# Pooling over rows: add two accumulators on the Vector engine first, then one set of matmuls in place of two

## What is computed

```python
def _forward(x, Wr, br, w1, b1, w2, b2, Wp1, bp1, Wp2, bp2):
    ...
    for e in range(E):                       # 12 experts, top 3 for each token
        ...
        out = out + mask[..., None].astype(x.dtype) * (w_e * h)
    pooled = out.mean(axis=1)                # mean over the 512 tokens of each batch
    phi = jax.nn.sigmoid(jax.nn.relu(pooled @ Wp1 + bp1) @ Wp2 + bp2)
    phi_mask = (phi > 0.7).astype(out.dtype)[:, :, None]
    return out * (1.0 - phi_mask * 0.8)
...
x = x + 0.5 * _L0_ffn_ref(_layernorm(x, axis=-1), ...)
x = x + _L0_attn_ref(_layernorm(x, axis=-1), ...)
x = x + 0.5 * _L0_ffn_ref(_layernorm(x, axis=-1), ...)
```

## Time and profile before

| | us |
|---|---|
| median of 3 runs | 842.14 |
| lowest and highest run | 838.91 to 844.8 |
| the profiled execution | 843.17 |
| its span, first to last instruction | 841.3 |
| PE busy | 695.0 (83% of the span) |
| DVE busy | 532.5 (63%) |

### The profile page before, as it was taken

The page is one execution under the profiler, slowest core; times in us unless marked ns, Lnnn a source line. Parts: engine busy times, 40 slices in busy tenths (PEclk is TensorE's granted clock), DMA queues, the critical chain, the costliest instruction groups (busy, mean ns, idle before and its releaser), DMA issues.

```text
span 841.3 us, 20947 instructions
## 1 busy us (share of the span) xinstructions
PE 695.0 (83%) x6530; PEld 589.0 (70%) x6531; DVE 532.5 (63%) x1085; ACT 313.9 (37%) x704; POOL 422.6 (50%) x302
## 2 busy tenths in 40 slices
PE   1416799999999998659999974179999999999964
PEld 1315687789889997238888863159999999989822
DVE  6895899745555555169899889835555555555505
ACT  3886677433333332022232221243333333333300
POOL 0003488888888885111100100137888888888520
PEclk9757999999999999769999995579999999999977
DMA  9987543656555654710000003043444444444473
GB/s 304 376 312 235 153 70 63 145 99 112 94 112 94 113 94 63 219 50 2 1 0 0 2 1 101 6 133 57 75 75 75 75 75 75 75 75 75 56 211 114
DMA packets 76803, 85.51 MB, mean 102 GB/s; under 512 B 7008, under 2 KB 68448, under 8 KB 76384
## 3 DMA queue, kind: packets, MB, share of 16 engines
q0 software_dynamic: 26880, 36.72, 26.8%
q1 hardware_dynamic: 49888, 48.35, 17.7%
HBM read 50.97 MB, written 34.08 MB: 101 GB/s over the span
## 4 chain that ended last, share of the span: by engine, by line
PE 61%; DVE 11%; issue 10%; DMA 8%; POOL 5%; SPq 3%; ACT 1%; DVEq 0%; ACTq 0%; POOLq 0%
PE PS L796 57%; POOL expert_sums L528 3%; PE PS L853 3%; DMA expert_sums<-zeros 3%; DMA A<-xn_rows,token 2%; DVE A L1335 2%; POOL A L509 2%; DMA W<-w 1%; SPq L432 1%; DMA A<-expert_sums 1%; DVE A L1332 1%; DMA expert_sums<-A,place 1%; DVE A L1539 1%; ACT A L630 1%; DVE A L1246 1%
## 5 line engine op out<-in xcount | busy, mean ns | idle before, releaser
L796 PE MATMUL PS<-A,W 128*128 128x256 f16 (+1 forms) x2356 | 279.1, 277 | 4.0 <-issue 2.2
L796 PE MATMUL PS<-W,A 128*128 (+1 forms) x2228 | 275.2, 280 | 5.6 <-issue 2.4
L509 POOL DMA_INDIRECT A<-xn_rows,token x140 | 177.7, 1270 | 192.7 <-DVE token L1358 123.9
L528 POOL DMA_INDIRECT expert_sums<-A,place x140 | 231.7, 1655 | 64.5 <-issue 40.4
L796 PEld LDWEIGHTS PS<-A,W 128*128 (+1 forms) x2356 | 238.5, 110 | 32.7 <-issue 6.4
L796 PEld LDWEIGHTS PS<-W,A 128*128 128x128 f16 (+1 forms) x2228 | 225.7, 103 | 37.0 <-issue 8.6
L706 ACT ACTIVATE A<-PS,b1s 128x256 f32<-128x256 f32 x340 | 131.5, 478 | 179.2 <-PE PS L796 179.2
L1392 DVE CAST A<-A 128x1280 f16<-128x1280 f32 x68 | 56.5, 831 | 198.0 <-ACT A L706 197.9
L1394 DVE TENSOR_TENSOR A<-A 128x1280 f16<-128x1280 f32 x68 | 101.5, 1493 | 2.3
L796 PE MATMUL PS<-A 32*128 32x128 f32 (+3 forms) x1248 | 66.7, 283 | 31.9 <-DVE A L1335 23.3
L699 ACT ACTIVATE A<-PS 128x512 f16<-128x512 f32 x70 | 41.9, 599 | 114.4 <-PE PS L853 114.3
(11 more groups left out here) (162 smaller groups left out, 430.9 us busy)
## 6 DMA issues: line engine op xcount, KB each, us to landing
W<-w SPq DMA_DIRECT2D x24, 640.0 KB, 11.1
A<-expert_sums SPq DMA_DIRECT2D x16, 512.0 KB, 6.2
expert_sums<-zeros SPq DMA_DIRECT2D x2, 2304.0 KB, 19.0
expert_sums<-zeros SPq DMA_DIRECT2D x12, 384.0 KB, 2.7
xn_rows<-A SPq DMA_DIRECT2D x8, 512.0 KB, 7.1
A<-b SPq DMA_DIRECT2D x2, 1536.0 KB, 8.4
A<-xn_rows,token POOLq DMA_INDIRECT x140
expert_sums<-A,place POOLq DMA_INDIRECT x140
```

The source lines that it names most:

```text
L509: nc.gpsimd.indirect_dma_start(XG[q][:, u * D:(u + 1) * D], None, xn_dram[:, :], bass.IndirectOffsetOnAxis(ap=token[:, at:at + 1], axis=0) ...
L528: nc.gpsimd.indirect_dma_start(sums_dram[f][q][:, :], bass.IndirectOffsetOnAxis(ap=place[:, at:at + 1], axis=0), YO[q][:, u * D:(u + 1) * ...
L796: return nc.tensor.matmul(out_, l, r, start=start, stop=stop_, skip_group_check=True)
```

## The change

PE no longer pools each lane by itself. It waits for DVE's add of a chunk (a new semaphore, `sums_added`, which counts up with every add) and pools the sum with 4 matmuls for each chunk, 16 in all. DVE's adds wait for both lanes' loads of their chunk and for nothing else. `pool_psum` is counted up once, after the last matmul, and DVE waits for it ahead of L1488. The loads and their order stay, as does all that follows L1488.

```diff
@@ combine, PE @@
-                for lane, sums in ((1, O2), (0, O)):
-                    for c in range(NC):
-                        pe.wait_ge(sums_in[lane][c], 16 * (f + 1))
-                        for b in range(B):
-                            ins = matmul(bank[1][0:B, 0:D], of_batch[:, b, :], sums[:, c * B + b, :],
-                                         lane == 1 and c == 0 and b == 0, lane == 0 and c == NC - 1 and b == B - 1)
-                        ins.then_inc(pool_psum, 1)
+                for c in range(NC):
+                    pe.wait_ge(sums_added, NC * f + c + 1)
+                    for b in range(B):
+                        ins = matmul(bank[1][0:B, 0:D], of_batch[:, b, :], O[:, c * B + b, :],
+                                     c == 0 and b == 0, c == NC - 1 and b == B - 1)
+                ins.then_inc(pool_psum, 1)
@@ combine, DVE @@
                 for c in range(NC):
                     for lane in range(LANES):
                         dve.wait_ge(sums_in[lane][c], 16 * (f + 1))
-                    dve.wait_ge(pool_psum, 2 * NC * f + NC + c + 1)
-                    v.tensor_tensor(Oc[:, c], Oc[:, c], O2c[:, c], ALU.add)
+                    v.tensor_tensor(Oc[:, c], Oc[:, c], O2c[:, c], ALU.add).then_inc(sums_added, 1)
+                dve.wait_ge(pool_psum, f + 1)
```

More of the change, by code:

```diff
@@ L354, in build @@
         marked = sem("marked")
+        sums_added = sem("sums_added")
         pool_psum = sem("pool_psum")
```

## The result

| | median us | lowest to highest | runs | ratio to the kernel before, 95% interval |
|---|---|---|---|---|
| kernel before | 843.28 | 838.91 to 845.34 | 20 | |
| changed kernel | 840.73 | 837.92 to 843.07 | 20 | 0.9974 (0.9962 to 0.9985) |
| changed kernel, again | 842.27 | 839.88 to 843.53 | 12 | 0.9982 (0.9961 to 1.0003) |
| changed kernel, again | 840.15 | 836.14 to 843.07 | 12 | 0.9966 (0.9941 to 0.9991) |

A forecast was written before the change was run, and what follows sets the result against it. Expert-block matmuls hold 57% of the chain, unchanged; in the combines PE, not DMA, ends last. Per combine +8.0 (later start) - 6.8 (matmuls) - 1.14 (add off the end) = +0.1 us, so 842.2 us, range 838 to 846 us.

The forecast's parts named there:

- PE's first pooling record later, counted from the last scatter's issue: Each combine: the first matmul waits for both lanes of chunk 0 and one add, starting 8.0 us later.
- burst: PE's pooling matmuls in each combine: 32 of 64 records go, all at full clock, saving 6.8 us.
- add off the end: Between last pooling matmul and L1488: the last add no longer stands there, giving back 1.14 us per combine.
- last matmul to the next DVE instruction: End of each combine's pooling: L1488 comes 0.12 us after the last matmul, as the add did before.
- The adds behind the first are hidden: DVE's adds 1 to 3 in each combine: hidden behind matmuls, so PE never waits for an add after the first.
- the 5% that I had allowed above it: DVE's adds while loads still write: 1.23 us each, with 5% (0.06 us) allowed above.
- rival 3: Pooling in each combine: PE pauses between chunks and its clock rises late, giving 845.7 us; chance 0.12.
- rival 4: Pooling in each combine: PE's clock doesn't rise at all, 4.1 us more each, 850.4 us; chance 0.03.
- Rival 1: Pooling in each combine: time simply halves, slow part included, to 8.2 instead of 9.6 us, 839.4 us; chance 0.13.
- Rival 2: Pooling in each combine: PE at full clock from the start keeps pace with landings, -3.5 us each, 835.2 us; chance 0.02.
- All behind L1488 is as before: After the pooling in each combine: everything following L1488 takes its old time, a change of 0 us.
- The net near zero: Both combines: later start, fewer matmuls and removed add nearly cancel, +0.1 us per combine, 842.2 us; chance 0.70.

The follow-up runs named there:

- the two warm bursts: Changed kernel plus unread matmuls keeping PE busy: ten after the last expert block, three at each lane 1 landing; 837.10 us, ratio 0.9927 to the kernel before.
- before, warm: Kernel before plus ten unread matmuls on a constant after the last expert block, last add in its old place; 837.36 and 838.99 us, ratios 0.9930 and 0.9948.

## Why the prediction was right and wrong

Averages over all profiles of the two kernels as they are (four combines before, six after), in us for each combine:

| term | predicted | measured |
|---|---|---|
| PE's first pooling record later, counted from the last scatter's issue | +8.0 | +8.1 (12.93 against 4.81) |
| burst | -6.8 | -7.2 (9.07 against 16.31) |
| add off the end | -1.14 | -1.14 |
| last matmul to the next DVE instruction | 0.12, as before | 0.04, so -0.1 |
| L1488 to gate | 0 | -0.4 (2.70 against 3.11) |
| sum | +0.1 | -0.76 (24.74 against 25.50) |

The rows give -0.76 but for their rounding. Twice that is -1.5 us, 0.9982 of 843 us. The three measured ratios, 0.9974, 0.9982 and 0.9966, have that value in their intervals; the last lies 1.3 us beyond it, which these profiles don't place. Against the forecast each combine is some 0.9 us shorter: 0.4 from the small matmuls, 0.4 from the burst, 0.1 from the step between PE and DVE.

**What held.** The start moved by the wait for lane 0 plus one add, within 0.1 us. The adds behind the first are hidden, and they take 1.22 to 1.23 us with the loads still writing, too (the adds at 351.61 and 353.36 above), so the 5% that I had allowed above it weren't needed. PE doesn't wait between chunks, which puts rival 3 aside; the clock does rise in the burst, which puts rival 4 aside. Rival 1 fell with the doubled matmuls. Rival 2 didn't happen in the changed kernel, and its condition could be made to happen: with PE at full clock from the start the burst is 7.1 to 7.55 us. Its price was too high, though. From a start at 818.8 us the 32 records at 0.213 us alone end at 825.6, later than the 824.9 that I let the last landing set, so it would have been 2.8 us less in each combine and not 3.5; the two warm bursts are bounded in the main by PE's own work.

**The step that failed** is the sentence "All behind L1488 is as before". I had the row that speaks against it within reach: the granted clock is a state that the small matmuls take over from what PE did before them. I counted what the add keeps waiting (1.14 us) and not what the wait does to the clock of the next matmuls. In the kernel before, with 2.3 us between the burst and them, the first small group took 1.02, 1.01, 0.61 and 0.90 us; with 1.0 us between, in the changed kernel, 0.61 six times of six. With the late add in the kernel before it was 0.61 four times of four, with the pause put back into the changed kernel 1.02 and 0.84. But with the warm matmuls and the add in its old place it was 0.61 four times of four in spite of the pause. So a pause of 2.3 us makes the fall likely and doesn't force it; shown is how often, not a limit. The Trainium skill, "TensorE: Matmul & The Clock Gate", "Why this matters for your kernels", advises against idle gaps between bursts of matmuls because the clock falls back in them. The trace agrees with the advice in kind; but the gaps that the Trainium skill warns of there are longer than this one, so by it the pause would have passed as harmless, where the trace shows the clock lost or partly lost after 2.2 to 2.3 us in 5 combines of 6 without warm matmuls.

**The mis-sized term** is the burst, by 0.4 us. Nearly half a us for each combine came from the moment at which the clock rose, about 4.1 us after the start on average in the changed kernel (worked back from the lengths of the bursts) against 5.0 in the kernel before. Over all kernels with a cold start the same working gives 3.0 to 5.9 us (bursts of 64 records from 15.30 to 16.77 us, of 32 from 8.64 to 9.61), so with six and four combines this difference may be chance. Nor do the experiments settle it: all ten bursts that start behind the add (those of the kernels with the pause and with doubled matmuls included) give 4.2 us on average, all eight that start with lane 1 give 4.8, each with a spread of 0.8 to 0.9. The Trainium skill, "TensorE: Matmul & The Clock Gate", Part 1, says that the number of slow matmuls differs from run to run of one kernel; the trace agrees, with 9 slow starts in one combine of the changed kernel and 12 in the other. I had 4.7 and 5.0 us from one execution and let two rows that agreed stand for a fixed value.

**The net near zero** was forecast for the right reason. The kernel before had half of its pooling under the wait for lane 0, and the change gives that cover up to save work that is worth little less than the cover was. Of the change's parts only one pays, the add off the end with what hangs on it, and it can be had without the rest.

## What to carry to other kernels

Before work is halved, look at what it lies beside: matmuls that run while a load is on its way cost little or nothing on the chain, and putting the engine behind the load instead trades them for idle time. Take small work off the chain between the last matmul of a burst and the next matmuls; it costs its own time and often the clock of what follows. And where PE has long been idle ahead of a burst on the critical chain, a few matmuls that nobody needs, issued right behind the last real ones, were worth more here than the change itself: 0.4% by the stretches with the late add and in the changed kernel, 0.5 and 0.7% by the times of "before, warm", a part of which stays unexplained.

## What the runs showed of the hardware that was not expected

- The same six small matmul records took 1.60 us at 0.50 and 1.00 us at 1.00 granted clock. A pause of 2.2 to 2.3 us ahead of them cost the full clock, wholly or partly, in 5 of 6 combines without warm matmuls, and in none of 4 with them; with a pause of 1.0 to 1.2 us the first group had it every time (12 of 12).
- A burst of the same matmuls after some 7 or 15 us of idle time rose to full clock anywhere between about 3.0 and 5.9 us after its start (worked back from the lengths of 18 bursts), which moves the end of a burst by 1.5 us from one execution to the next.
- In the changed kernel DVE starts L1488 0.03 to 0.04 us after the burst's end; in the kernel before its add started 0.12 us after it, with a wait of DVE's queue at L1486 (0.05 us, from 827.29) as a piece of its own in the chain. I had taken the 0.12 us over.
- PE's clock also fell in waits of only 2.4 to 3.3 us behind a long busy stretch, in three combines out of ten with the further matmuls.
